# Softmax row sums computed one quarter ahead, expert rows gated on GpSimd and added on VectorE, and two band writes queued together

## The reference, cut to what matters

```python
# attention over a window of 64 positions, 16 heads of width 8
strain = disp_win - disp[:, :, :, None, :]
logits = bond_logits(strain) - 10.0 * sigmoid(damage(strain))
weights = softmax(where(cmask, logits, -inf), axis=-1)       # over the 64 of the window
out = einsum('bntd,bntde->bnte', weights, val_win) @ W_cproj
# mixture of experts on the same normalised x: 16 experts, the best 4 of each token
acc = sum over the 4 chosen experts of  route[token, expert] * y_expert[token]
x = x + out + x_n + acc
```

## Time and profile before

| | us |
|---|---|
| median of 3 runs | 1155.72 |
| lowest and highest of them | 1152.77, 1164.46 |
| the profiled execution, its own time | 1149.74 |
| its span, first to last instruction | 1147.7 |
| setup, 0 to 48.0 | 48.0 |
| item stage g = 0, to 299.0 | 251.0 |
| band stage g = 0, 299.0 to 380.8 | 81.8 (PE busy 57.7, DVE 57.8, ACT 46.0; granted clock 0.87) |
| item stage g = 1, to 630.2 | 249.4 |
| band stage g = 1, 630.2 to 716.3 | 86.1 (PE busy 63.0, DVE 68.8, ACT 36.0; granted clock 0.82) |
| second layer, to 1147.7 | 431.4 |

### The profile page before, as it was taken

One profiled execution on the slowest core, in us unless ns is written; L12 is line 12 of the kernel. 1 busy time (PEld: TensorE's weight loads), 2 busy tenths in 40 slices (PEclk: granted clock), 3 DMA queues, 4 the chain that ended last, 5 costly groups with the idle time before them and its releaser, 6 DMA issues. The chain is left out here.

```text
span 1147.7 us, 23697 instructions
## 1 busy us (share of the span) xinstructions
PE 976.7 (85%) x9302; PEld 524.1 (46%) x9302; DVE 915.4 (80%) x1062; ACT 789.4 (69%) x859; POOL 553.9 (48%) x563
## 2 busy tenths in 40 slices
PE   6778777798777899999987687998999999989897
PEld 4522222233466344433333576634746465555533
DVE  7897888899756999999996778678587668576857
ACT  3689999999754799999997642432266656565474
POOL 6098888738536458888886300507720000000172
PEclk9899999999988899999999788998799999999999
DMA  8880011111287222222210783000314344432121
GB/s 301 232 349 33 31 35 34 37 52 55 59 234 164 61 62 74 71 73 72 73 55 33 204 225 88 22 1 19 96 51 121 100 113 136 126 106 81 37 61 45
DMA packets 102598, 109.58 MB, mean 95 GB/s; under 512 B 11893, under 2 KB 87121, under 8 KB 98769
## 3 DMA queue, kind: packets, MB, share of 16 engines
q1 hardware_dynamic: 93492, 87.67, 26.4%
q0 software_dynamic: 7424, 20.20, 5.9%
q10 hardware_dynamic: 1571, 0.20, 0.1%
HBM read 62.29 MB, written 42.59 MB: 91 GB/s over the span
## 5 line engine op out<-in xcount | busy, mean ns | idle before, releaser
L262 DVE SCALAR_TENSOR_TENSOR ring<-AD,PT 128x1808 f32<-128x1808 f32 (+15 forms) x128 | 281.9, 2221 | 26.8 <-PE LG L980 25.8
L980 PE MATMUL LG<-ring,lred 128*32 128x456 f32 (+15 forms) x2048 | 233.3, 574 | 0.0
L268 POOL DMA_INDIRECT ys<-rows,goali x80 | 164.1, 2052 | 62.5 <-DVE rows L864 39.0
L2343 DVE TENSOR_REDUCE MX<-SS 128x2 f32<-128x1024 f32 x119 | 144.5, 1218 | 55.1 <-PE SS L2060 55.0
L2273 ACT ACTIVATE EX<-SS 128x1024 f32<-128x1024 f32 x128 | 130.4, 1031 | 81.5 <-PE SS L2060 80.9
L920 ACT ACTIVATE ring<-ring 128x3680 f32<-128x3680 f32 (+15 forms) x47 | 161.2, 3430 | 3.6 <-DVE ring L262 3.6
L1005 PE MATMUL SD<-DSf,eyes 99*32 99x456 bf16 (+15 forms) x1280 | 95.6, 375 | 69.6 <-ACT ring L925 66.6
L773 POOL DMA_INDIRECT xs<-rows,sloti x64 | 134.3, 2098 | 30.8 <-issue 19.2
L926 ACT ACTIVATE ring<-ring 128x1824 f32<-128x1824 f32 (+15 forms) x80 | 145.8, 1822 | 0.0
L1977 POOL DMA_INDIRECT XN<-ys,sloti x16 | 16.3, 1022 | 247.8 <-PE SS L2070 243.2
L262 DVE SCALAR_TENSOR_TENSOR ring<-AD,bdmg 128x1808 f32<-128x1808 f32 (+15 forms) x48 | 106.3, 2214 | 0.0
(11 more groups left out here) (432 smaller groups left out, 1716.4 us busy)
## 6 DMA issues: line engine op xcount, KB each, us to landing
w1s<-in_L_ffn_W SPq DMA_DIRECT2D x39, 256.0 KB, 3.0
w2s<-in_L_ffn_W SPq DMA_DIRECT2D x39, 256.0 KB, 3.0
band<-Z SPq DMA_DIRECT2D x8, 1024.0 KB
xl<-xs SPq DMA_DIRECT2D x20, 272.0 KB, 3.0
xs<-Z SPq DMA_DIRECT2D x5, 1024.0 KB, 8.9
w1s<-w1d SPq DMA_DIRECT2D x80, 64.0 KB
w2s<-w2d SPq DMA_DIRECT2D x80, 64.0 KB
ring<-band SPq DMA_DIRECT2D x12, 384.0 KB, 5.2
```

The lines of the kernel that those rows point to most:

```text
L262: return v.scalar_tensor_tensor(out=tile[:, s, :, t0:T], in0=AD[:, s, :, j + t0:j + T], scalar=extra, in1=AD[:, s, :, PAD + t0:PAD + T], o ...
L268: pool.indirect_dma_start(ys0[:, :], bass.IndirectOffsetOnAxis(ap=goali[:, 4 * n + a:4 * n + a + 1], axis=0), yo[:, n % 2, a, :], None, bo ...
L980: mm = pe.matmul(LG[32 * b:32 * b + 32, par, s, t0:T], lred[:, s, n % 4, :], ring[:, slot, s, b, t0:T], start=(n % 4 == 0), stop=(n % 4 == 3))
L2343: v.tensor_reduce(MX[:, t, p // 2, hh:hh + 2], pairs_of(b, name), AX.X, ALU.max).then_inc(freed[slot], 1)
```

## The change

Four edits. `sums(0)` stands ahead of quarter 0, and `sums(k+1)` where `sums(k)` stood; the two halves of `mx` take turns as the quotients' tile, and the reciprocal is taken in place. `add_rows` is cut in two: GpSimd multiplies eight tiles of fetched rows by their gates in place, in one instruction, and VectorE adds them in one `tensor_tensor`; GpSimd's products stand between its clears and reads, those of choices 2 and 3 after its last read. SyncE queues write 3 right behind write 2, ahead of read 2 and of `fetch(2)`. And one semaphore of the second layer, `nx_hi`, is replaced by the chain that VectorE's other instructions use.

```diff
 def add_rows(v, k, half):
-    v.wait_ge(d_yg[k % 2], (208 * G, 64 * GROUPS0)[k % 2] + 16 * (k // 2 + 1))
+    v.wait_ge(gated, 2 * k + half + 1)
     if k or half:
         v.wait_ge(added, 2 * k + half)
-    for t in range(8 * half, 8 * half + 8):
-        a = ACC[:, t, :]
-        ins = v.scalar_tensor_tensor(out=a, in0=yg[k % 2][:, t, :], scalar=gates0[:, k, t:t + 1], in1=a, op0=ALU.mult, op1=ALU.add)
-    ins.then_inc(added, 1)
+    r = slice(8 * half, 8 * half + 8)
+    v.tensor_tensor(ACC[:, r, :], ACC[:, r, :], yg[k % 2][:, r, :], ALU.add).then_inc(added, 1)
+
+def gate_rows(pool, k, half):
+    pool.wait_ge(d_yg[k % 2], (208 * G, 64 * GROUPS0)[k % 2] + 16 * (k // 2 + 1))
+    r = slice(8 * half, 8 * half + 8)
+    rows = yg[k % 2][:, r, :]
+    pool.tensor_tensor(rows, rows, gates0[:, k, r].unsqueeze(2).to_broadcast([P, 8, C]), ALU.mult).then_inc(gated, 1)
...
-            total, quotient = mx[:, 0, :], mx[:, 1, :]
+            quotients = (mx[:, 0, :], mx[:, 1, :])
...
                 clear(1)
+                if g == G - 1:
+                    gate_rows(pool, 0, 0)
+                    gate_rows(pool, 0, 1)
                 read(pool, 0, 1)
                 clear(2)
                 read(pool, 1, 1)
                 if g == 0:
                     store(pool, MOE[0][7][1])
+                else:
+                    gate_rows(pool, 1, 0)
+                    gate_rows(pool, 1, 1)
                 for k in range(2, NT):
                     read(pool, k, 1)
+                if g == G - 1:
+                    for k in range(2, K0):
+                        for half in range(2):
+                            gate_rows(pool, k, half)
...
                 for half in range(2):
                     sp.wait_ge(*landed(0, half))
+                write(2)
+                write(3)
                 for k in range(2, NT):
-                    write(k)
                     read(sp, k, 0)
                     if g == G - 1:
                         sp.wait_ge(added, 2 * k - 2)
                         fetch(sp, k)
...
                 def sums(k):
+                    q = quotients[k % 2]
                     v.wait_ge(ex_ready, 5 * g + k + 2)
-                    link(v.tensor_reduce(total, zs[k].rearrange("p s n -> p n s"), AX.X, ALU.add))
-                    v.reciprocal(quotient, total).then_inc(rc_ready, 1)
+                    link(v.tensor_reduce(q, zs[k].rearrange("p s n -> p n s"), AX.X, ALU.add))
+                    v.reciprocal(q, q).then_inc(rc_ready, 1)
...
                 for k in range(NT):
                     weigh(k)
+                sums(0)
                 if g == G - 1:
                     add_rows(v, 0, 0)
                 for k in range(NT):
                     turn(k)
-                    sums(k)
+                    if k + 1 < NT:
+                        sums(k + 1)
...
-                    pe.transpose(WB[0:32, 0, 0, :], quotient, ident[:]).then_inc(rct_pe, 1)
+                    pe.transpose(WB[0:32, 0, 0, :], quotients[k % 2], ident[:]).then_inc(rct_pe, 1)
...
-            v.tensor_scalar(nx[:, :, :, 24].bitcast(F32R), m, -1.0, None, ALU.mult).then_inc(nx_hi, 1)
-            v.wait_ge(nx_hi, b + 1)
+            link(v.tensor_scalar(nx[:, :, :, 24].bitcast(F32R), m, -1.0, None, ALU.mult))
```

More of the change, by code:

```diff
@@ L633, in first_layer @@
     d_yg = (d_parts, d_w2)
-    added = sem("added")
+    added, gated = sem("added"), sem("gated")
     sd_ready, sd_taken = sem("sd_ready"), sem("sd_taken")
@@ L1783, in values_bank @@
         return PN if slot_of(b, "v") == 2 else bank_of(b, "v")[:, 0, :]
-    hi_ready, nx_hi, nx_ready, inverted = (sem(n) for n in ("hi_ready", "nx_hi", "nx_ready", "inverted"))
+    hi_ready, nx_ready, inverted = (sem(n) for n in ("hi_ready", "nx_ready", "inverted"))
     nd_ready, nd_copied, at_ready = (sem(n) for n in ("nd_ready1", "nd_copied", "at_ready"))
```

## The result

The changed kernel took 1141.01 us in the median of 4 runs (1139.31 to 1147.3), the kernel before 1156.49 beside it: a ratio of 0.9877, 95% interval 0.9839 to 0.9915. Foreseen were 1136. The gain is some 14 us where 20 were forecast. Between the two profiled executions it is 10.4 (1149.74 to 1139.31).

What follows compares the result with a forecast made beforehand. Waits, not work, were taken to bound two band stages, chiefly TensorE's wait for VectorE's sums and reciprocal. 23.5 - 1.5 - 1.0 - 0.8 = 20.2, say 20 us; 1155.7 - 20 = 1136 us, range 1127 to 1148.

Steps and rivals of the forecast that it cites:

- All eight gaps: TensorE's waits for VectorE's reciprocal ahead of the quotients' transposes, both band stages: all close, 11.4 + 12.1 = 23.5 us gained.
- step (c): Last quarter, g = 0: VectorE's strains and ScalarE's activations end late; of 4.7 us some 3.9 arrive, 0.8 given back.
- Rival 3: In `gather`, another wait, for ScalarE's copy of the quotients, ends just behind the removed one; half of 23.5 stays, 1146; chance 0.08.
- (a): Transfers at turn 2: for g = 0 it waits for its table, 1.5 us given back; for g = 1 no loss.
- Write 3 ahead of read 2: SyncE's queue: SyncE's half of read 2 lands at about 348, worth nothing there; read 3 lands some 5 us sooner.
- rival 1: Joined write delays read 2: turn 2 late by 5.8 us (g = 0) and 4.4 (g = 1), total 1144.7; chance 0.14.
- the predicted losses together: Amounts given back from the closed gaps: 1.5 us for transfers, 1.0 for VectorE, 0.8 in the last quarter.
- The range: Whole kernel: from 1127 us, all 23.5 arriving and a better-held clock, to 1148, half the gain staying, both with scatter.
- (b): VectorE, g = 1, quarters 0 and 2: needs 13.8 us with old additions, 11.9 with new, against TensorE's 11.3; 1.0 given back.
- Products on GpSimd: GpSimd's gate products: 1.9 to 3.7 us each, 2.3 taken; costs nothing at 2.3, 2 to 4 us at 3.7.
- rival 4: Slower: GpSimd's product far dearer than its rows, holding up its reads from 5.1 us each; at 12 us, 1176; chance 0.04.
- Rival 2: VectorE's additions and GpSimd's products exclude each other in quarters 2 and 3: 5 to 7 us on VectorE, 1142; chance 0.12.

Runs made afterwards that it cites:

- the second profile: Changed kernel run once more, unaltered, beside other kernels on one chip: 1141.68 us; the kernel with only the sums moved, also run again, took 1142.39 us.
- light transfers: Changed kernel with band writes cut to 16 of 64 positions and reads to 16 of 95, same instructions: 1128.21 us in one run.
- the kernel with filler: Kernel before, with idle TensorE products in the gap ahead of each quotients' transpose, sums not moved: 1155.98 us, ratio to before 1.0001.
- the run with 32 products more: Changed kernel with 32 more idle TensorE products ahead of turn 0 of each stage: 1141.19 us in one run.
- warm kernel: Changed kernel with more idle TensorE products ahead of turns 0 and 2, where it waits for a table: 1144.52 us, ratio to before 0.9905.
- the fetches last: Changed kernel with SyncE's read 2 ahead of write 3 and both fetches behind read 3: 1146.86 us in one run.
- the gates alone: Kernel before with only GpSimd's gate products, VectorE's short additions and the semaphore's swap: 1154.1 us, ratio 1.0003.

## Why the prediction was right or wrong

**Right: which wait bounds, and what the edit does to it.** All eight gaps closed, 23.3 us of the 23.5. At the end of g = 0, of 4.7 us 3.9 were to arrive, and TensorE still waits 0.83 there; but it waits for ScalarE's copy, not for the strains that step (c) named, so the size of that price is luck. Rival 3 fell with this.

**Wrong: the landing of read 2, in (a) and in *Write 3 ahead of read 2*.** The second says that SyncE's half lands "at about 348, no later than GpSimd's did", and prices the edit at nothing; (a) counts 1.5 us for g = 0 and none for g = 1. Measured: a flight of 10.5 us instead of 4.9, GpSimd's last transfer 11.4 instead of 9.9, waits of 4.77 us at turn 2 of g = 0 and of 3.15 at that of g = 1, and 1.12 at turn 3. The argument that the same bytes flow and only their order changes was true, and did not help: TensorE waits for one of them. Its departure for write 3 was early by 1.0 us: the exp that it waits for started only half a microsecond sooner into the stage, since turn 0 ahead of it was slower. That did not hold read 2, which waited for write 2; write 3 was issued before write 2 landed, as the step says.

**Half right: rival 1.** What it foretold happened, at its places and nearly at its price (5.8 and 4.4 us late against 4.77 and 3.15), though with a flight of 10.5 us for SyncE's half, not 15.2, and with GpSimd's half late as well. But it is not the reason why the total fell short: with the writes in their old order the flight is back at 4.9 and the time is the same (1141.45). What TensorE no longer waits for the table it then loses to its own slower turns and pauses, and in g = 1 at turn 3. The other half of *Write 3 ahead of read 2* was right: write 3 first does bring read 3 early. With the sums alone and the old order, turn 3 waits 3.0 us in g = 0 and 6.6 in g = 1 for its table (second profile); in the changed kernel 0 and 1.1. So with the gaps closed the tables are late in either order, and the order only says at which turn. Only the tables' whole traffic taken away brought "to turn" down, to 8.1.

**Not foreseen: pauses of TensorE inside its groups, 6.1 us** (3.7 in the second profile). That is nearly twice the predicted losses together (3.3). By these runs they are waits for TensorE's instructions: each ends 1.2 to 1.7 us after a 16 KB packet of the instruction queue, their places go with the program (32 and 28 products earlier for 32 and 28 put in), and with light transfers they fall to 1.1. The kernel before has none because its packets come just in time, and its gaps of 2.2 to 4.7 us are what gives them that time: in the kernel with filler, where these gaps are full of products, 7.0 us of pauses appear. What sets the moment at which a packet is moved stays open; in the run with 32 products more, TensorE had stood for 2.1 us when the packet started.

**Not foreseen: the clock.** The range allowed for a better granted clock in fewer gaps, down to a gain of 28. It does hold better in the gathers (10.9 us), and falls in the turns (8.4, of which the 1.4 of turn 0 in g = 0 is scatter between executions). The kernel with filler has the same clock in the gathers, 1.00, and 1.0001 of the time before, so the gathers' clock alone brings nothing; part of why is the pauses. The mean granted clock of the span was 0.951 before, and 0.950 to 0.954 in the changed, the filled and the warm kernel. What sets it at one place and not at another stays open.

**Wrong in (b): that the old additions would keep the gaps open.** It says that with them VectorE needs 13.8 us in quarters 0 and 2 of g = 1, and "most of those gaps would stay". The sums alone, with the old additions, close them all: "to quotients" is 15.0 as in the changed kernel, and no wait on VectorE's reciprocal is left. The 1.0 us that (b) gives back was not seen either: the changed kernel's turns wait for no copy of VectorE in the first profile, and for 0.6 us in the second. TensorE's cycle in g = 1 is not the 11.3 us of the step but 11.7 to 16.6, with the waits for tables and pauses in it.

**Sizes in (b) and *Products on GpSimd*.** The addition (1.22) and the product (1.87, at the low end of 1.9 to 3.7, with 2.3 taken) are as sized, and rival 4 falls with the product. Rival 2 is real and small: two additions that should take 2.4 us took 4.18, since the first met a product, once in the stage, and the next copy started at 697.91, 0.8 us after its transposes ended at 697.07. The 5 to 7 us of the rival needed three or four such meetings. That each can hold the other up is in the traces: the addition that began beside the product took 2.85 us instead of 1.22, and with the fetches last two products that began beside an addition took 2.87 us each instead of 1.89. The edit as a whole is worth nothing measurable here (1.0003 alone), since VectorE is not what TensorE waits for.

**The sum.** Put with measured terms: -23.3 of gaps, +8.5 of waits for tables, +6.1 of pauses, -2.5 of clock, +0.2 elsewhere: -11.0, where -20 stood. The stages took 75.4 and 81.3 us, where 72 and 75 were named. Outside the two stages the first item stage ended 2.15 us later and the second layer took 1.1 less, so 10.1 between the two spans. The medians of the runs differ by more, 14 us by the ratio; how much of the 3 to 4 us between is scatter of single executions (the second profile of the changed kernel has 1.5 us less in the stages than the first) stays open. The forecast of 1136 was 5 us low, and the range held.

## What to carry to other kernels

When a transfer is put ahead of another in one queue, price the second with the first in front of it (here 10.5 us, not the 4.9 that it took before), even where the bytes in flight stay the same; and where a gap on the bounding engine is closed, one run with small transfers shows how much of a second bound behind it is transfers (here 16.0 us of 156.7). The gaps here also hid things that no wait in the profile names, a lower clock behind them (0.53 to 0.61 in the gathers, 1.00 with the gaps gone) and pauses in the supply of instructions (none with the gaps, 6.1 us without); a ledger of the stage cut at fixed points of the program, beside that of the changed kernel, finds them where the list of waits does not. And edits that only relieve an engine nobody waits for should be expected to bring nothing, however much work they save it (1.0003 for the gates alone).

## What the runs showed of the hardware

TensorE stood for 0.2 to 4.6 us in the middle of groups of products, by these runs waiting for its own instructions: all 38 such pauses of the fourteen profiles ended 1.2 to 1.7 us after a 16 KB packet of the instruction queue had ended, and one of them moved 32 and 28 products up the program for 32 and 28 put in ahead. They made 6.1 us beside full transfers and 1.1 beside small ones. The granted clock of one and the same stretch differed between two executions of one program: turn 0 of g = 0 ran at 1.00 and took 3.83 us in one profile of the changed kernel, and at 0.70 and 5.29 us in the other. Filling the gap ahead of it took a gather from 0.55 of the clock to 1.00 and from 3.74 to 2.20 us, and brought nothing in the whole (1.0001); the mean over the span stayed within 0.950 to 0.954. A VectorE addition with both inputs in SBUF took 2.85 us beside a GpSimd product and 1.22 alone, and a GpSimd product 2.87 us where it began beside such an addition and 1.89 otherwise. One issue of a transfer on SyncE (673.06, g = 1) took 9.78 us with read 2, issued at 668.47, still under way (turn 2 waited for it until 681.58), against 1.08 for the pair of write 3 in g = 0, and the fetch behind it in that queue left only at 684.21.
